# Local attention: the value product placed directly behind the query-key projection on TensorE

## What is computed

```python
qkv = x @ Wqkv                                  # x with half its features shifted by one token
q, k, v = (sh(t) for t in jnp.split(qkv, 3, -1))
q, k = l2norm(q) * qs, l2norm(k) * ksc          # then rotary tables with a growing scale
sim = jnp.einsum('bhwie,bhwje->bhwij', bq, bk2) * QK_SCALE   # own window and the one before
attn = jax.nn.softmax(jnp.where(mask, -jnp.finfo(sim.dtype).max, sim), -1)
out = jnp.einsum('bhwij,bhwje->bhwie', attn, bv2)
x = out.reshape(b, n, INNER) @ Wo + x
```

## Time and profile before

| | us |
|---|---|
| median of three runs | 5836.69 |
| lowest and highest of them | 5811.36, 5860.56 |
| profiled execution, its own time | 5868.65 |
| its span in the profile | 5866.9 |

### The profile page before, as it was taken

The page is one execution under the profiler, slowest core; times in us unless marked ns, Lnnn a source line. Parts: engine busy times, 40 slices in busy tenths (PEclk is TensorE's granted clock), DMA queues, the critical chain, the costliest instruction groups (busy, mean ns, idle before and its releaser), DMA issues. The chain is left out here.

```text
span 5866.9 us, 143623 instructions
## 1 busy us (share of the span) xinstructions
PE 5284.4 (90%) x46548; PEld 3143.6 (54%) x46548; DVE 4178.8 (71%) x8715; ACT 3627.3 (62%) x10714; POOL 3415.1 (58%) x3696
## 2 busy tenths in 40 slices
PE   7999999999999985799999999799999999999997
PEld 4656656665665652233434433466566656566564
DVE  6888888888888872343434343788888888888885
ACT  4777777777777760022222222677777777777785
POOL 6877777777777761000001000777777777777774
PEclk8999999999999995587979787899999999999998
DMA  2121121211112111000000000212111121111111
GB/s 66 39 53 41 42 52 37 54 41 50 45 36 53 42 31 21 0 1 1 1 1 1 1 1 1 67 37 53 41 49 45 37 53 42 49 44 39 51 41 30
DMA packets 266274, 203.85 MB, mean 35 GB/s; under 512 B 76284, under 2 KB 263192, under 8 KB 264728
## 3 DMA queue, kind: packets, MB, share of 16 engines
q1 hardware_dynamic: 265496, 194.08, 13.0%
HBM read 41.87 MB, written 1.05 MB: 7 GB/s over the span
## 5 line engine op out<-in xcount | busy, mean ns | idle before, releaser
L528 POOL TENSOR_TENSOR rot<-t 128x512 f32<-128x512 f32 x768 | 972.9, 1267 | 860.6 <-DVE t L816 418.4
L523 POOL TENSOR_TENSOR inv<-ssm,neg_half 128x8 f32<-128x8 f32 x768 | 1325.3, 1726 | 0.0
L710 ACT ACTIVATE prob<-ps,nmx,inv 128x96 f32<-128x96 f32 x3072 | 1278.6, 425 | 0.6
L593 PE MATMUL ps<-w_qkv,xs 128*128 128x512 f32 x1536 | 877.5, 654 | 63.1 <-issue 30.9
L1267 ACT ACTIVATE ptl<-ps_l 128x1024 f32<-128x1024 f32 (+1 forms) x288 | 281.4, 977 | 968.0 <-PE ps_l L1142 735.7
L697 ACT COPY vt<-ps 128x256 f32<-128x256 f32 x768 | 286.4, 373 | 785.5 <-PE ps L629 785.5
L660 PEld LDWEIGHTS ps<-pt,vs 96*64 96x64 f32 x12288 | 427.2, 139 | 388.4 <-issue 351.6
L629 PE MATMUL ps<-w_qkv,xs 128*128 128x256 f32 x1536 | 549.7, 440 | 89.3 <-ACT ots L678 87.1
L825 DVE TENSOR_SCALAR ssm<-ss 128x8 f32<-128x8 f32 x768 | 595.6, 775 | 26.4
L710 ACT ACTIVATION_READ_ACCUMULATOR prob<-ps,nmx,inv 128x1 f32 x3072 | 608.2, 198 | 0.0
L816 DVE TENSOR_TENSOR t<-ps,tab_s 128x256 f32<-128x256 f32 x1536 | 575.1, 416 | 0.0
(11 more groups left out here) (203 smaller groups left out, 8891.5 us busy)
## 6 DMA issues: line engine op xcount, KB each, us to landing
vs<-vt SPq DMA_DIRECT2D x768, 96.0 KB, 2.2
vs<-vt SPq DMA_DIRECT2D x768, 64.0 KB, 2.1
vs<-vt SPq DMA_DIRECT2D x768, 32.0 KB, 1.8
w_qkv<-in_L_ffn_Wqkv SPq DMA_DIRECT2D x48, 384.0 KB, 3.5
w_o<-in_L_ffn_Wo SPq DMA_DIRECT2D x12, 512.0 KB, 4.0
w<-in_L_ffn_W SPq DMA_DIRECT2D x12, 341.0 KB
wcos<-const_wc SPq DMA_DIRECT2D x2, 1024.0 KB, 4.9
wsin<-const_ws SPq DMA_DIRECT2D x2, 1024.0 KB, 7.3
```

Of the source, the lines that this page charges most:

```text
L523: nc.gpsimd.tensor_tensor(inv[:, n % 4], ssm[:, n % 2], neg_half[:, 0:2 * HU], ALU.pow).then_inc(z["inv_ready"], 1)
L528: nc.gpsimd.tensor_tensor(rot[:, n % 4], t1[:, n % 2], t2[:, n % 2], ALU.add).then_inc(z["rotated"], 1)
L593: pe.matmul(ps[:, j % 2, :], xs[:, j // UT % 2, :], w_qkv[:, 0:2, u * 256:(u + 1) * 256], start=True, stop=True).then_inc(z["qk_ready"], 1)
L710: e = nc.scalar.activation(prob[:, n % 2, h, :], scores[:, h % 2, h // 2, :], ACT.Exp, scale=inv[:, n % 4, h:h + 1], bias=nmx[:, n % 2, h: ...
```

## The change

TensorE's value product (L629) with its two waits moves from behind the scores to directly behind the query-key projection, in front of the layer output and the scores. The instruction, its operands, what it waits for and the other engines' programs stay as they are.

```diff
--- before.py
+++ after.py
@@ -592,6 +592,14 @@
                         pe.wait_ge(z["t2_ready"], 2 * done(0, 2))
                     pe.matmul(ps[:, j % 2, :], xs[:, j // UT % 2, :], w_qkv[:, 0:2, u * 256:(u + 1) * 256],
                               start=True, stop=True).then_inc(z["qk_ready"], 1)
+                if live(LAG_V):
+                    n = (j - LAG_V) % 8
+                    if had(LAG_V, 1):
+                        pe.wait_ge(z["v_read"], done(LAG_V, 1))
+                    if had(LAG_O, 1):
+                        pe.wait_ge(z["ot_read"], done(LAG_O, 1))
+                    pe.matmul(ps[:, 6, 0:256], xs[:, n // UT, :], w_qkv[:, 2, (n % UT) * 256:(n % UT + 1) * 256],
+                              start=True, stop=True).then_inc(z["v_ready"], 1)
                 if live(LAG_Y) and (j - LAG_Y) % UT == UT - 1:
                     tile = (j - LAG_Y) // UT
                     pe.wait_ge(z["ot_read"], done(LAG_Y))
@@ -620,14 +628,6 @@
                             mm = pe.matmul(scores[q0s:q0s + STRIP, b, r, :], qkt[h0:h0 + 64, n, r, WIN + q0s:WIN + q0s + STRIP],
                                            qkt[h0:h0 + 64, n, 2 + r, q0s:q0s + SKEYS], start=False, stop=True, skip_group_check=True)
                     mm.then_inc(z["s_ready"], 1)
-                if live(LAG_V):
-                    n = (j - LAG_V) % 8
-                    if had(LAG_V, 1):
-                        pe.wait_ge(z["v_read"], done(LAG_V, 1))
-                    if had(LAG_O, 1):
-                        pe.wait_ge(z["ot_read"], done(LAG_O, 1))
-                    pe.matmul(ps[:, 6, 0:256], xs[:, n // UT, :], w_qkv[:, 2, (n % UT) * 256:(n % UT + 1) * 256],
-                              start=True, stop=True).then_inc(z["v_ready"], 1)
                 if live(LAG_P):
                     n = (j - LAG_P) % 8
                     pe.wait_ge(z["weighted"], done(LAG_P))
```

## The result

| | us |
|---|---|
| before, median of 4 runs | 5824.02 (5787.62 to 5860.56) |
| with the change, median of 4 runs | 6184.34 (6170.24 to 6241.48) |
| ratio | 1.0616, 95% interval 1.0568 to 1.0664 |
| profiled execution with the change, its own time | 6194.28 |
| its span | 6192.5 |

The change makes the kernel 6.2% slower. 6183 was forecast, inside a range of 6080 to 6300.

What follows compares the result with a forecast made beforehand. Each slot was taken as the longer of a TensorE-ScalarE loop (4.69 us) and TensorE's own work; the period's slots summed to 95.7 us against 88.5, 346 us over 48 periods, giving 6183 from the median 5836.69, range 6080 to 6300.

Steps and rivals of the forecast that it cites:

- The loop: Plain slots: value product waits for ScalarE's copy `ots`, so the loop over TensorE and ScalarE goes from 4.69 to 5.05 us.
- The layer output: Slots with a layer output: it now lies between value product and transposes, adding 1.78 us: 6.83 against 6.47 or 5.62.
- VectorE, p = 5: Slot 5 of the 16-slot period: VectorE's two instructions of the slot before overrun 5.05 us, 0.6 taken, bounds nothing and 1.2.
- ScalarE's extras: Between `qkt` and `ots`: `f_src` adds 0.6 us, gelu with table 2.79; the exponentials' table adds 1.42 one slot later.
- The clock: Gelu slots: longer TensorE wait brings the 1.2 GHz level sooner, 1.0 us a period, bounds zero and 1.5.
- The sum: Whole 16-slot period: 95.7 us against 88.5, so 7.2 more, over 48 periods 346 us, giving 6183.
- B: Rival, faster: `ots` always copied before the product is due, loop 4.15 us, 156 us saved, about 5681; chance 0.02.
- C: Rival, no change: TensorE's own work, 81.44 of 87.58 us a period, covers everything, 5837; chance 0.04.
- D: Rival, clock falls in four more slots a period, 1.15 us each, 221 us in all, about 6400; chance 0.07.

Runs made afterwards that it cites:

- old order without gelu: Kernel before the change (value product behind the scores) with an Identity in place of the gelu, both table loads gone: 5720.93 us, ratio 0.9829.

## Why the prediction was right, point by point

- **The loop.** 5.05 us forecast, 5.05 measured in plain slots, released by the end of `ots`, as the run with the doubled copy shows by a cost of 0.28 us a slot. The wait in front of the product was forecast at about 1.2 us and some 700 in all, and was 0.99 and 556.9. The path by its parts, forecast and measured: to the transposes 1.29 and 1.26, to `pt` 0.64 and 0.67, to `qkt` 2.13 and 2.13, to `ots` 0.46 and 0.46, copy 0.39 and 0.39, to the product 0.14 and 0.14.
- **The layer output.** 6.83 forecast, 6.84 measured, 1.78 us inside the loop. The run with the layer output in front shows it as a cause of its own, 2.0 of the 7.0 us.
- **VectorE, p = 5.** This term was mis-sized: 0.6 forecast, nothing measured, the lower bound. VectorE after the change in these slots (timeline):

```profile
872.41 0.73 DVE L758 SCALAR_TENSOR_TENSOR f_sc<-f_xc,vec,ps 128x512 f32<-128x512 f32 x1
873.18 0.51 DVE L760 TENSOR_SCALAR f_xn<-f_sc,vec 128x512 f32<-128x512 f32 x1
873.61 0.17 DVE L782 RECIPROCAL rec<-sums 128x4 f32<-128x4 f32 x1
873.81 0.56 DVE L784 TENSOR_TENSOR prob<-prob,rec 128x384 f32<-128x384 f32 x1
...
874.89 0.55 DVE L800 TENSOR_REDUCE mx<-ps 128x4 f32<-128x384 f32 x1
```

  From L782 to the maxima it needed 1.28 us and not the 1.55 of the earlier trace rows, because the weighting took 0.56 here; the one in the stretch that I had read took 0.82. The pair L758, L760 costs 1.20 up to the next instruction, not 1.29. The forecast's own figures did not fit either: 4.40 and 0.75 make 5.15, more than the 5.05 into which they were said to fit just. So the maxima start 1.53 us behind the product (873.36), 0.17 later than in plain slots, which the slack in front of the exponentials takes. With a loop of 4.57 us the same work did cost 0.5, though by the weighting, for which the transposes waited, and not by the maxima.
- **ScalarE's extras.** `f_src` 0.6 forecast, 0.52 measured (p = 0 takes 5.57). The gelu: p = 8 forecast 7.84, measured 7.91 on average.
- **The clock.** This term was mis-sized the other way: 1.0 us a period forecast, 1.38 measured: p = 9 takes 7.85 on average, and 5.05 and the table's 1.42 make 6.47. The two gelu slots (windows) and the product between them:

```profile
890.30:898.14 7.84, 4.01 (x47) 2.55 (x47) 5.25 (x11) 7.06 (x17) 6.09 (x6) 0.97 0.10 25
898.14:906.10 7.96, 7.85 (x48) 4.56 (x49) 4.30 (x10) 5.17 (x15) 3.96 (x6) 0.60 0.12 29
```

```profile
898.14 1.19 PE L601 MATMUL ps<-w_qkv,xs 128*128 128x256 f32 x2 [3.83 <-ACT ots L678]
```

  TensorE stood still for 3.83 us and then ran the product at the 1.2 GHz level, 1.19 us instead of 0.67, with a mean granted clock of 0.60 over the slot; most periods show about 0.79 for slots of nearly the same length. The kernel before pays for the clock as well, 0.7 us by the estimate above, so about 0.7 of the 1.4 belongs to the change.
- **The sum.** A period of 95.7 us forecast, 95.47 measured: the two misses, 0.6 too much and 0.4 too little, nearly cancel. Then I multiplied the difference of 7.2 us by 48. In the profiled executions the stacks together became 329 us longer, 346 forecast, and the whole span 325.6 (6192.5 less 5866.9); the first and last few slots of a stack are not full periods. From the medians the difference is 360 us, ratio 1.0616. That the forecast hit the median to within 2 us is thus partly luck: the profiled execution of before lay 45 us above the median as it is now, that of the changed kernel 10. The latent attention, whose time varies as the experiments show, is one source of such differences.
- **The rivals.** B (faster, if `ots` is always copied in time) fell as it stood, but its mechanism is real: with `ots` ahead of `qkt` the plain loop is 4.57 us. C fell. D (more falls of the clock) fell: plain slots with 0.99 us of waiting in 5.05 kept their durations.

## What to carry to other kernels

When an instruction is moved up in one engine's queue, look at the place of its releaser in the other engine's queue: the wait that comes along was free only as long as something else stood in front of it, and here a copy one place behind the former releaser made each pass of a loop over two engines 0.36 us longer. Everything put between the waiting instruction and the step that the other engine waits for is in the loop: the 1.78 us of layer output, which had been worked off while ScalarE did the slot before, now lengthened the loop four times a period, and that place alone cost 2.0 us of the 7.0. And find the loop by its releases, slot by slot, rather than by busy shares: in the changed kernel TensorE is 86% busy, and its own work sets the length of one slot in 16 (p = 12, 6.42 us).

## What the runs showed that I had not expected

- The stretch between the stacks, most of it latent attention, took 1434 to 1577 us in the 13 profiled executions, with the mean granted clock between 0.83 and 0.74; the code of the attention is the same in all of them. That spread of 143 us is larger than several of the effects looked for. In the kernel before, the granted clock was 0.50 over 100 us of it (2431 to 2531) in which TensorE's rows fill 95.6 us.
- A wait of 2.42 us ahead of the product was enough for TensorE's clock to fall to the 1.2 GHz level (granted 0.73 over the next slot, the run without gelu), and at 1.5 us a period that cost as much as the wait of 3.83 us in the changed kernel (1.4). Waits of 0.99 us in each plain slot of the changed kernel did not bring it down. But the length of this one wait does not decide it: in the old order without gelu the clock fell in 7 periods of 36 behind a wait of 0.90 us that was the same in all of them.
- Durations on VectorE go with what GpSimd does at the time. The clamp L825 on 128x8 elements takes 0.75 us while GpSimd's addition L528 runs; it ends 0.03 us after that addition does (872.50 and 872.47). At the start of the stack, ahead of the addition, it took 0.17. VectorE and GpSimd in the changed kernel (timeline):

```profile
65.37 0.17 DVE L825 TENSOR_SCALAR ssm<-ss 128x8 f32<-128x8 f32 x1
...
871.75 0.75 DVE L825 TENSOR_SCALAR ssm<-ss 128x8 f32<-128x8 f32 x1
```

```profile
65.67 1.26 POOL L528 TENSOR_TENSOR rot<-t 128x512 f32<-128x512 f32 x1
...
871.20 1.27 POOL L528 TENSOR_TENSOR rot<-t 128x512 f32<-128x512 f32 x1 [0.45 <-DVE t L816]
```

  The Trainium skill (SBUF — State Buffer, Who interferes with whom) says that the two engines share a port pair, which one holds for a whole instruction while the other waits, if VectorE's instruction runs in one of its two-port modes, or has two inputs in SBUF and GpSimd's reads SBUF. The clamp's row agrees with such a wait; the mode in which it ran stands in no row. In the kernel before, the clamp started while a GpSimd instruction ran in 766 of 768 cases, and took 0.17 us in only 36 of these.

  The weighting L784 took 0.56 us in all 241 cases of the kernel before in which it ran beside L523 alone, and 0.82 in the stretch of the earlier trace rows, beside L497 and L498. A duration of this engine read in one slot is therefore not a constant of the kernel, and that is how the VectorE term above was mis-sized. These are coincidences in the trace: no run here separated the two engines.
